# A graph layer with routed experts: the output bias as a row of the mix matrix, token routing in four groups with scattered slots, and gathered pairs 9 and 18

## The reference, cut to what matters

```
xn = layernorm(x)
x  = x + gnn(xn) + mix(xn)
x  = x + ffn(layernorm(x))

gnn: h = xn * rsqrt(deg_out); agg = segment_sum(h[src], dst)
     h = relu(agg * rsqrt(deg_in) @ W + b); h / norm(h)
mix: q, k, v = heads(xn @ w_qkv.T); k, v normalized per head
     dots = k.T @ v;  (q @ dots / N) @ w_out.T + b_out
ffn: logits = h @ gate_w + gate_b; idx = argmax; prb = softmax(logits)[idx]
     pos = cumsum(one_hot(idx)) - 1;  kept = pos < C   (8 experts, C = 977)
     buf[idx, pos] = h; y = (relu(buf @ w1 + b1) @ w2 + b2)[idx, pos] * prb * kept
```

## Time and profile before

| what | value |
|---|---|
| runs | 1472.56, 1465.79, 1465.27 us; median 1465.79 us |
| profiled execution | 1463.94 us, with a span of 1462.7 us |
| PE busy, share of the span | 1305.0 us, 89% |
| DVE busy | 1198.4 us, 82% |
| ACT busy | 934.8 us, 64% |
| POOL busy | 799.2 us, 55% |
| mean granted TensorE clock | 0.970 |

### The profile page before, as it was taken

One profiled execution on the slowest core, in us unless ns is written; L12 is line 12 of the kernel. 1 busy time (PEld: TensorE's weight loads), 2 busy tenths in 40 slices (PEclk: granted clock), 3 DMA queues, 4 the chain that ended last, 5 costly groups with the idle time before them and its releaser, 6 DMA issues. The chain is left out here.

```text
span 1462.7 us, 38776 instructions
## 1 busy us (share of the span) xinstructions
PE 1305.0 (89%) x14051; PEld 1091.4 (75%) x14053; DVE 1198.4 (82%) x2455; ACT 934.8 (64%) x2122; POOL 799.2 (55%) x629
## 2 busy tenths in 40 slices
PE   4698888995879999998989998999999898989987
PEld 3355555562768888887878887888886687979986
DVE  7797888898869888998899888989984577767786
ACT  4486777776546676665756666657665556565754
POOL 5357445206238888888888884000000577676574
PEclk8799999997989999999999999999999999999999
DMA  9625431002826655666655664121114433343220
GB/s 301 209 57 118 93 77 37 29 23 93 255 64 114 120 99 99 99 99 131 107 105 122 108 101 75 38 73 38 38 38 138 126 118 122 95 136 116 74 79 25
DMA packets 96441, 145.71 MB, mean 100 GB/s; under 512 B 14249, under 2 KB 72262, under 8 KB 96123
## 3 DMA queue, kind: packets, MB, share of 16 engines
q0 software_dynamic: 46080, 69.85, 26.0%
q1 hardware_dynamic: 50186, 73.61, 15.1%
HBM read 105.08 MB, written 60.14 MB: 113 GB/s over the span
## 5 line engine op out<-in xcount | busy, mean ns | idle before, releaser
L1688 PE MATMUL bank<-reg_b,reg_a 128*128 128x256 f16 x4410 | 597.3, 275 | 8.5 <-ACT reg_a L1277 8.0
L1277 ACT ACTIVATE reg_a<-bank 128x392 f16<-128x392 f32 x720 | 343.0, 496 | 214.7 <-PE bank L1680 187.2
L1688 PEld LDWEIGHTS bank<-reg_b,reg_a 128*128 128x128 f16 x4410 | 396.8, 98 | 51.0 <-issue 10.2
L976 POOL DMA_INDIRECT reg_a<-h_rows,reg_d x216 | 395.1, 1829 | 66.2 <-issue 66.2
L1964 DVE TENSOR_TENSOR reg_c<-iota_v,reg_c 128x2048 f16<-128x2048 f16 (+1 forms) x282 | 368.2, 1321 | 45.3 <-ACT reg_c L1170 15.6
L1680 PE MATMUL bank<-reg_a,reg_c 128*128 128x98 f16 x2880 | 243.0, 209 | 16.1 <-ACT reg_a L1277 10.2
L1680 PEld LDWEIGHTS bank<-reg_a,reg_c 128*128 128x128 f16 x2880 | 200.4, 99 | 32.4 <-issue 17.4
L1964 DVE TENSOR_TENSOR reg_a<-iota_h,reg_c 128x1568 f16<-128x1568 f16 x180 | 174.3, 968 | 0.0
L990 POOL COPY take_idx<-inv_i 128x8 int32<-128x8 int32 (+1 forms) x8 | 1.7, 217 | 240.5 <-DVE inv_i L2515 240.5
L1920 PE MATMUL bank<-w_hi,hid_hi 128*128 128x256 f32 (+1 forms) x368 | 107.3, 292 | 12.1 <-DVE w_lo L2550 6.9
L1922 PE MATMUL bank<-w_hi,hid_lo 128*128 128x256 f32 (+1 forms) x368 | 104.6, 284 | 0.0
(11 more groups left out here) (370 smaller groups left out, 2520.6 us busy)
## 6 DMA issues: line engine op xcount, KB each, us to landing
reg_b<-in_L_ffn_w SPq DMA_DIRECT2D x16, 1024.0 KB
h_rows<-reg_b POOLq DMA_DIRECT2D x14, 896.0 KB, 9.8
tok_rows<-reg_e SPq DMA_DIRECT2D x24, 512.0 KB
x_bias<-in_x SPq DMA_DIRECT2D x1, 6250.0 KB
x_bias<-b_out_rows POOLq DMA_DIRECT2D x10, 625.0 KB
x_t<-x_bias SPq DMA_DIRECT2D x24, 256.0 KB
xnT_t<-xnT_rows SPq DMA_DIRECT2D x24, 256.0 KB
out<-reg_e SPq DMA_DIRECT2D x24, 256.0 KB
```

Of the source, the lines that this page charges most:

```text
L976: ins = g.indirect_dma_start(out=acc[i % 2][m][k], out_offset=None, in_=h_rows, in_offset=at, compute_op=ALU.add)
L1277: return a.activation(AT[k].rearrange("p h (w t) -> p h w t", w=2)[:, :, :, s * GROUP:(s + 1) * GROUP], tile_ps[bk][:, 0:GROUP * 2 * NB].r ...
L1688: ins = t_.matmul(agg_ps[k][:, 0:D], AT[k][:, h, :], h_all[:, half, h, :], start=(first and h + half == 0), stop=(last and h == NB - 1 and ...
```

## The change: what it does

1. **Bias.** `x_bias`, its 6250 KB copy, the bias rows and the ten accumulating transfers go; pairs load x itself. `b_out` is divided by the mix matrix's column norms (which now include b_out squared), scaled and split into two f16 halves, and is held in two rows of a 128x256 tile. For each block PE adds one more matmul of 256 columns, with a left operand that has two nonzero rows. Five short DVE instructions join the preparation of the mix matrix, three memsets POOL's.
2. **Routing in groups.** For each pair only the scaling of the gate logits stays on DVE (one instruction). The rest is done for pairs 0 to 7, 8 to 15, 16 to 21 and 22, in a dense block each (the 19th, 33rd and 43rd position) and in the tail. A group is 9 and 11 DVE instructions over up to 16 blocks, one exponential on ACT, and on PE 17, 17, 13 and 3 matmuls. The last 3 blocks keep the old way.
3. **Slots by scatter.** POOL writes (node, probability) pairs of 8 bytes to a DRAM table `slot_rows`, one indirect transfer of 128 rows for each of 46 blocks, behind the gathers on its queue. The table is cleared early by a 64 KB store. In the tail SP waits for all 46, loads the table (64 KB), and `add_slots` adds it once to the place matmul of the last blocks. The wait before the key transposes falls away, save for one after each group.
4. **Gathered pairs** are 9 and 18 instead of 8 and 16.

```diff
-ROUTE_STEPS = 11
+FIN_STEPS = MIX_STEPS + 1
+GROUP_STEPS = 17
+ROUTES = ((0, 8), (8, 16), (16, 22), (22, 23))
-GATHERED = (8, 16)
+GATHERED = (9, 18)
...
-        sp.dma_start(x_bias.rearrange("(p j) d -> p (j d)", p=XB_ROWS), x.rearrange("(p j) d -> p (j d)", p=XB_ROWS)
-                     ).then_inc(xb_in, 16)
+        sp.wait_ge(inv_added, 1)
+        sp.dma_start(slot_rows.rearrange("(p c) w -> p (c w)", p=P), inv_acc[:, :]).then_inc(slots_clear, 16)
...
-            sp.dma_start(x_t[:, :, :], pair_rows(x_bias, q)).then_inc(x_ld, 16)
+            sp.dma_start(x_t[:, :, :], pair_rows(x, q)).then_inc(x_ld, 16)
...
         load_b2(0, 0)
+        sp.wait_ge(placed, 16 * 2 * (NQ - 1))
+        sp.dma_start(slot_tab, slot_rows.rearrange("(p c) w -> p c w", p=P)).then_inc(w_in2, 16)
         finished(NQ)
...
-            if i == 0 and XB_FROM <= q < XB_FROM + XB_PARTS:
-                bias_rows(q - XB_FROM)
...
+        def scatter(b):
+            g.indirect_dma_start(out=slot_rows, out_offset=bass.IndirectOffsetOnAxis(ap=slot_row[:, b:b + 1], axis=0),
+                                 in_=token[:, b, :], in_offset=None, bounds_check=NE * CROWS - 1, oob_is_err=False
+                                 ).then_inc(placed, 16)
+        def group(i):
+            pool.wait_ge(slot_hot, i + 1)
...
+                    t_.matmul(o.mix_ps[:, m, :], b_out_at, b_out_hl, start=True, stop=False)
...
+        def group(i, keys=None):
+            w = 2 * (ROUTES[i][1] - ROUTES[i][0])
+            pe.wait_ge(key_out, min(keys or 2 * ROUTES[i][1] + 3, NB))
+            pe.wait_ge(route_hot, i + 1)
+            t_.matmul(cum_ps[:, 0:w, :], utri16[:, :], g_hot[:, 0:w, :], start=True, stop=False)
+            for d in range(1, w):
+                t_.matmul(cum_ps[:, d:w, :], ones16[:, :], g_hot[:, 0:w - d, :], start=False, stop=False)
+            t_.matmul(cum_ps[:, 0:w, :], ones16[:, :], g_routed[:, 0:w, :], start=False, stop=True).then_inc(route_cum, 1)
...
-                            pe.wait_ge(inv_added, placed + 1)
-                            if counted:
-                                pe.wait_ge(slot_hot, counted)
+                        if place_ < 0 and p - 1 in group_pos:
+                            pe.wait_ge(slot_hot, group_pos.index(p - 1) + 1)
...
                 dve.wait_ge(fin_gate, q + 1)
-                choose(q, q)
+                v_.tensor_tensor(logits[:, ds(q * 2, 2), :], gate_ps, mix_bc[:, D:DG].unsqueeze(1).to_broadcast([P, 2, NE]),
+                                 ALU.mult).then_inc(gate_out, 1)
...
+            group_step(v_.tensor_scalar(low, slot, P - 1, None, ALU.bitwise_and))
+            group_step(v_.tensor_scalar(high, slot, 7, None, ALU.arith_shift_right))
+            group_step(v_.scalar_tensor_tensor(low, low, float(NE * CT), high, ALU.mult, ALU.add))
+            group_step(v_.tensor_tensor(slot_row[:, b0:b1], low, drop, ALU.add))
+            dve.sem_inc(slot_hot, 1)
```

More of the change, by code:

```diff
@@ L512, in build @@
     gs_of = [g_s if q in (0, NQ - 2, NQ - 1) or q % 2 == 0 else g_alt for q in range(NQ)]
[L514 to L518, removed]
+    KEYS_AT, MIX_AT = 2, 9
+    GroupAt = namedtuple("GroupAt", "choose exps count route")
+    GROUP_AT = GroupAt(0, 6, 8, 8)
+    group_pos = [-(-(starts[q1 - 1] + 2 * SLOTS) // SLOTS) for _, q1 in ROUTES[:-1]]
+    gs_of = [g_s if q in (0, NQ - 2, NQ - 1) or q % 2 == 0 else g_alt for q in range(NQ)]
+    KEYS_AT, MIX_AT = 2, 9
+    GroupAt = namedtuple("GroupAt", "choose exps count route")
+    GROUP_AT = GroupAt(0, 6, 8, 8)
+    group_pos = [-(-(starts[q1 - 1] + 2 * SLOTS) // SLOTS) for _, q1 in ROUTES[:-1]]
     def places_of(q):
-        return PLACES[(KEYS_AT - starts[q]) % SLOTS]
+        return Places(9, 11, 12) if (KEYS_AT - starts[q]) % SLOTS == 10 else Places(9, 9, 8)
     def active(p, s):
@@ L525, in active, with main_phase @@
         return [(q, at - starts[q]) for q in range(NQ - 1) if 0 <= at - starts[q] < 2 * SLOTS]
-    def main_phase(eng, gnn, prepare, first, second, tail, sparse, ahead=None):
+    def main_phase(eng, gnn, prepare, first, second, tail, sparse, group, ahead=None):
         def blocks(with_rounds):
@@ L541, in pairs @@
             pair(0)
-            with eng.Fori(1, NQ - 2) as q:
-                pair(q)
+            for i, (q0, q1) in enumerate(ROUTES[:-1]):
+                with eng.Fori(max(q0, 1), q1) as q:
+                    pair(q)
+                group(i)
             pair(NQ - 2)
@@ L693, in pair_rows @@
             if blocks_of(q) == 1:
-                n = LAST if rows is x_bias or rows is out else P
+                n = LAST if rows is x or rows is out else P
             rows = rows[ds(first, n), :]
@@ L932, in h_part @@
                     pool.wait_ge(h_pool, t - H_POOL[0])
+        chain(g.memset(b_out_at, 0.0))
+        for half in range(2):
+            chain(g.memset(b_out_at[half * 64:half * 64 + 1, :], HSCALE))
         pool.wait_ge(deg_ok, 1)
@@ L979, in sparse @@
                         landed[i % 2][m][k] += 1
[L981 removed]
+            for i in range(len(ROUTES) - 1):
+                group(i)
+        main_phase(pool, gnn, lambda b, s: None, lambda q, s: None, lambda q, s: None, tail, sparse, group)
         pool.wait_ge(agg_done, NB)
@@ L1805, in tail @@
             last_rounds = rounds_of(pe, NB - 1)
-            for s in (5, 6):
-                first(NQ - 1, s)
+            first(NQ - 1, 6)
+            group(len(ROUTES) - 1)
             pe.wait_ge(tile_out, NB * SLOTS + len(tile_ps))
@@ L2328, in first @@
                 biased(q, *(sums or ()))
-                if not sums:
-                    slots_of_last(q)
+                n[0] = 0
             if c == 3:
-                if not first_pair(q) and not fixed(q, NQ) and not sums:
-                    add_slots(q - 1)
                 if not fixed(q, NQ):
@@ L2458, in tail @@
             dve.wait_ge(fin_gate, NQ + 1)
-            choose(NQ - 1, NQ, 3, last_route)
-            route(NQ - 1, NQ, 3, last_route)
-            add_slots(NQ - 1)
+            last_choose()
+            last_slots()
+            add_slots()
         def sparse():
```

316 lines of the change are left out of this document (176 added, 140 removed).

## The result

| kernel | runs | median us | ratio to before | 95% interval |
|---|---|---|---|---|
| before | 9 | 1466.89 | | |
| changed | 9 | 1458.22 | 0.9953 | 0.993 to 0.9975 |

Forecast: 1406 us, a ratio of 0.959. The change made the kernel faster, but by 9 us in place of 57, and the range from 1393 to 1430 did not hold the time. The profiled execution of the changed kernel took 1463.23 us with a span of 1461.9 us, at the slow end of its runs (1454.03 to 1466.79), so its stage times are read against before with some 5 us of doubt.

The account below looks back on a forecast made before the run. PE was taken as the bound in the second stage, working 71.11 of 73 us. Terms 11 + 3 + 4.7 + 15.5 + 10.0 + 8.5 - 1.5 + 5.9 = 57.1 us off 1463.9 gave 1406.8, stated as 1406; range 1393 to 1430.

Parts of the forecast that it names:

- part 3, the scatters: POOL after its last accumulating gather: 46 indirect transfers take 69 us there, hidden by 3 to 6 us of cover; taken 0.
- copy of x: First stage, SP's queue: without the copy the store lands before ACT wants it; PE gains 11 us.
- ten transfers: First stage, 109 to 201 us: removing the accumulating bias transfers lets PE issue faster; 3 us, half the 6.4 bound.
- waits before key transposes, late DVE, clock: Stage two, PE: key waits gone 15.5 us, gaps behind late DVE statistics 10.0, low clock behind gaps 8.5.
- groups' own cost: Stage two, DVE: each group adds 2 us to its block, three times; 0.5 us lost each, so -1.5.
- late gathers: Stage two: with pairs 9 and 18 gathered rows arrive in time, removing 5.9 us of PE's gaps.
- PE's work 4.7: PE: count and place matmuls removed 13.1 us, bias matmuls add 5.9 and group matmuls 2.5; 4.7 us gained.
- tail 0: Tail: DVE gets pair 22's group in place of `route` and a wait for `place`; -1 to +1 us, taken 0.
- A (DVE late): Stage two: groups put 5.6 us in one block, so the statistics stay late; 22 us less gain, 1428; chance 0.15.
- B (store held): First stage: input loads on SP's queue still hold the first store, so the 11 becomes 0: 1417; chance 0.10.
- C: Tail: slow scatters make the slot table 201 us late, 1607; chance 0.04 for slower, 0.02 for nothing left.
- D: Whole kernel: bias transfers worth all of 6.4, tail 1, groups free; 6 us more gain, 1400; chance 0.07.

Follow-up runs that it names:

- threes: Changed kernel with a wait for the landing after every fourth scatter and after every third first-stage gather: 1411.14 us, 0.9604 of before.
- part 1 alone: Kernel before with only the bias change, routing and gathered pairs as before, run twice: 0.9955 (1452.35 us) and 0.9962 of before.
- pairs816: Changed kernel with the gathered pairs set back to 8 and 16: 1467.34 us, 1.0058 of before.
- none: Changed kernel without its 46 scatters and without SP's wait for them, slot table left unfilled: 1366.78 us, 0.9584 of before.
- paced: Changed kernel with POOL waiting for each scatter to land before issuing the next: 1380.78 us, 0.9677 of before.
- the first four: Changed kernel without scatters, with waits after each or every fourth scatter, or with reads for writes: 0.9584, 0.9677, 0.9589, 0.9585 of before.
- after_third: Changed kernel, not edited, run again on another chip than the first result's: 1450.34 us, 0.9927 of before.
- triple: Changed kernel with each scatter of the first two groups issued also to two spare tables, 96 in place of 32: 1532.7 us, 1.0509 of before.
- mixed: Changed kernel with waits after every fourth of the first 32 scatters and the third group's 12 as reads in a row: 1428.62 us, 0.975 of before.
- fours_u: Changed kernel with a wait for the landing after every fourth scatter: 1428.4 us, 0.9724 of before.

## Why the prediction was wrong

**The step that failed** is part 3, the scatters: "69 us on POOL, which has no other work after its last accumulating gather", and "Taken: 0". It measured 0 on the quick chip and some 37 us, by the matmul counts below, on the first. The cover was worked out for POOL's own queue and for the slot table's due time. Both held: in the changed kernel `add_slots` waited 1.10 us for its matmul and not for the table. What was not asked is what a row of POOL's transfers does to the other engines. On the chip of the result it costs them nearly the time of the row, from about 17 us into it (902.8 to 920): with 221 matmuls in 18 us as the rate, 348 are missing from 920 to 951, 28 us, and against 443 in the kernel before 111 from 1060 to 1097, 9 us. The rule that was weighed there, about 2.0 us for each DMA in the Trainium skill ("DMA: Bandwidth & Descriptors", Anatomy of one DMA), was not the danger: the scatters came every 1.28 us. The other half of it, that transfers under 512 bytes are read, modified and written (the Trainium skill, "DMA: Bandwidth & Descriptors", Specifications), no run here prices: 12 reads of such rows cost PE 6.2 us and 12 writes 6.5, but that is the stall. (The cover for it was given as about 197 us; the figures worked out below it, 1080 - 881, make 199.)

**A sign was there.** The earlier trace rows has 961 matmuls in 92 us and 550 in the 49 behind. I read the difference as the bias transfers' price. But the changed kernel, without them, does 929 in the same 92 us on that chip, and on the quick chip they stand beside 1178. From 146 to 220 us the kernel before has this wait of PE, which the prediction did not ask about:

```profile
PE bank L1484 <- issue: 6.6, 14, 0.5
```

These are gaps without a releaser beside POOL's rows of gathers, as later beside the scatters. That the gathers make them is shown in part, by threes.

Point by point, with the quick chip as the case without the stall:

| step | forecast us | measured |
|---|---|---|
| copy of x | 11 | no wait for the store left; PE 8.2 us ahead at 73 us (28.95 - 20.79), 6.2 at the start of stage two (392.8 to 386.5) |
| ten transfers | 3 | 0.0 from 73 to 146 us, beside the first five (71.38 and 71.39 busy); -0.2 from 109 to 201 (89.68 and 89.91 without them) |
| part 1 alone, 11 + 3 - 5.9 | 8.1 | on the first kind: 6.6 and 5.6 (ratios 0.9955 of 1459.7, 0.9962 of 1464.4) |
| waits before key transposes, late DVE, clock | 15.5 + 10.0 + 8.5 | the waits of the earlier trace rows gone on both kinds; clock 1.00 in the quick chip's second-stage windows shown |
| groups' own cost | -1.5 | no gap at the first three: on the quick chip PE is busy 365.0 of 365 us from 440 to 805, the first among them; 1.3 us at the one in the tail |
| late gathers | 5.9 | 17.0 (pairs816, on the first kind), with 14 us less of the scatters' stall in it |
| scatters | 0 | 0 seen on quick chips (none 0.9584 on one, changed 0.9589 on another); some 28 + 9 us and the clock on the first kind |
| PE's work 4.7, tail 0 | 4.7 | not measured by themselves |

From the first gather of stage two to the first list of the third stage, the kernel before took 706.9 us on the quick chip (392.8 to 1099.7) and the changed one 660.1 (386.5 to 1046.6): 46.8 us less, where the terms behind the first stage said 43.1. Two terms were off in opposite ways, the first stage by 8 too much on this chip (14 against 6.2; on the first kind part 1 came out near its term) and the gathers by 11 or more too little, as far as a price from the other kind of chip carries over, so the sum of 57 met the measured 58 of the quick chip partly by luck. Single waits (keys, DVE, clock, PE's work, the tail) were not tried one at a time; only their sum is shown.

On the first chip the same stretch went from 713.0 us to 707.4, so 41 us of those 47 were missing there; the matmuls counted above give 37 of them, and the low clock is in the same windows. The stage behind it took 328.4 us in place of 324.4, which no run explains.

The Trainium skill ("DMA: Bandwidth & Descriptors", Queues, rings and completion order) says that each DMA engine takes its queues in turn, a packet at a time. By it the ten transfers should have been worth next to nothing, and the quick chip's windows agree (71.38 and 71.39 us busy); I took half the bound from rows instead.

The rivals: A (DVE late) and B (store held) didn't occur: neither wait is left. C did not occur in the changed kernel, but its mechanism appeared in paced. D had the bias transfers at 6.4 us, and they were worth nothing that shows. None of them had POOL slowing the other engines, which is why the range failed.

## What to carry to other kernels

"Engine X is idle here, so the work costs nothing" needs a second question: what does its work take from the others? A long row of indirect transfers from POOL deserves a break (here a wait for the landing after every fourth, which cost nothing where it wasn't needed), but not where someone waits for the rows. And a result from one chip is one chip's: run the unedited changed kernel beside each experiment; the first four here lacked it.

## What the runs showed of the hardware that was not expected

- On two chips (those of the result and of after_third and triple) PE, ACT and DVE issue almost nothing while POOL issues indirect transfers 1.28 us apart, from some 16 to 17 us into the long row: 66 matmuls in 102 us, DMA share 0.06, so it is not the bandwidth of the transfers. The row of 12 costs PE some 6 us, from about 7 us into it, and so it does on a third chip (mixed). A fourth (threes, fours_u) has the thin first stage. On three other chips there was no sign of it; on the one where the changed kernel itself ran, PE is busy 73 of 73 us beside the scatters. What the engines share here is not shown, nor whether a chip always stays of its kind; one met twice was quick both times.
- Beside the accumulating gathers, 2.1 us apart, PE works 437.4 of 438 us in the changed kernel on the first chip, and with a break after every fourth scatter (32 in some 64 us, 2.0 each) its gaps are 1.9 us from 900 to 970 (fours_u). In a row the 32 came 1.39 us apart. In pairs816, with one break after 16, they came 1.63 us apart and most of the stall was gone. Whether the mean spacing or the length of the row decides was not told apart.
- On the quick chip it is POOL that takes longer: of its 46 scatters the longest took 4662 ns and the first 32 lasted from 864.7 to 920.1 us, against 1710 ns and 902.8 to 946.9 on the first.
